# Rotary embedding of queries and keys: the swapped halves copied by DMA inside SBUF, with a signed sine table, instead of multiplied by a permutation matrix

## What is computed

```python
x = rms_norm(hidden_states, ln_in_w)
mixed = jnp.where(vm, x @ v_qkv, x @ l_qkv)
q, k, v = jnp.split(mixed, 3, axis=-1)
...
def rotate_half(x):
    d = x.shape[-1] // 2
    return jnp.concatenate([-x[..., d:], x[..., :d]], axis=-1)
...
q, k = q * cos + rotate_half(q) * sin, k * cos + rotate_half(k) * sin
```

## Time and profile before

| | us |
|---|---|
| median of three runs | 2036.79 |
| lowest and highest | 2032.74 and 2040.6 |
| the profiled execution | 2036.72 |
| its span | 2034.9 |
| PE busy | 1918.8 |
| DVE busy | 1113.8 |
| POOL busy | 887.1 |
| ACT busy | 830.2 |

### The profile page before, as it was taken

One profiled execution on the slowest core, in us unless ns is written; L12 is line 12 of the kernel. 1 busy time (PEld: TensorE's weight loads), 2 busy tenths in 40 slices (PEclk: granted clock), 3 DMA queues, 4 the chain that ended last, 5 costly groups with the idle time before them and its releaser, 6 DMA issues.

```text
span 2034.9 us, 35472 instructions
## 1 busy us (share of the span) xinstructions
PE 1918.8 (94%) x12620; PEld 1642.6 (81%) x12620; DVE 1113.8 (55%) x2663; ACT 830.2 (41%) x2198; POOL 887.1 (44%) x1037
## 2 busy tenths in 40 slices
PE   4999979997999999999999999998979999999998
PEld 3876767775999989888899879985458888887997
DVE  6777875666442553547676554222384766655422
ACT  2017526875211211256666423222235666652321
POOL 3340322341798999641121348840044212104884
PEclk9999988999999999999999999998989999999999
DMA  3110100010233333310000213322221000001332
GB/s 127 42 57 2 40 15 16 30 50 17 83 109 109 115 114 124 88 35 18 11 24 13 67 63 104 114 73 88 70 80 34 19 10 24 13 1 42 104 113 79
DMA packets 38190, 118.88 MB, mean 58 GB/s; under 512 B 6168, under 2 KB 10264, under 8 KB 38016
## 3 DMA queue, kind: packets, MB, share of 16 engines
q1 hardware_dynamic: 31408, 107.92, 17.3%
q10 hardware_dynamic: 6608, 8.68, 1.4%
HBM read 114.75 MB, written 1.84 MB: 57 GB/s over the span
## 4 chain that ended last, share of the span: by engine, by line
PE 82%; DVE 7%; POOL 5%; ACT 2%; issue 2%; DMA 1%; DVEq 0%; ACTq 0%; SPq 0%; POOLq 0%
PE psum L565 15%; PE psum L566 14%; PE psum L567 14%; PE psum L787 7%; PE psum L798 6%; PE psum L845 5%; PE psum L558 4%; PE psum L685 4%; PE psum L687 4%; PE psum L686 4%; POOL wl L1701 3%; DVE xc L1277 1%; DVE rstd L1262 1%; ACT probs_t L1042 1%; DVE total L1248 1%
## 5 line engine op out<-in xcount | busy, mean ns | idle before, releaser
L1701 POOL TENSOR_TENSOR wl<-raw,wh 128x256 fp32r<-128x256 f32 x656 | 518.9, 822 | 13.7
L565 PE MATMUL psum<-nh,wh 128*128 128x448 f32 x904 | 348.3, 385 | 15.3 <-DVEq L1477 8.0
L1693 POOL TENSOR_SCALAR wh<-raw 128x1024 fp32r<-128x1024 f32 x164 | 185.1, 1129 | 396.8 <-PE psum L567 158.4
L566 PE MATMUL psum<-nl,wh 128*128 128x448 f32 x904 | 336.9, 373 | 0.0
L567 PE MATMUL psum<-nh,wl 128*128 128x448 f32 x904 | 336.3, 372 | 0.0
L1042 ACT ACTIVATE probs_t<-masked_t,nmin 112x375 f32<-112x375 f32 (+1 forms) x384 | 202.6, 529 | 109.2 <-DVE nmin L1380 109.2
L1549 DVE TENSOR_TENSOR hid_l<-scr,hid_h 128x448 fp32r<-128x448 f32 x108 | 93.2, 863 | 229.0 <-ACT hid_h L1129 228.4
L565 PEld LDWEIGHTS psum<-nh,wh 128*128 128x128 f32 x904 | 174.7, 193 | 37.6 <-issue 12.5
L1380 DVE CUSTOM_DVE_ANT_0 masked_t<-psum,maskf 112x375 f32<-112x375 f32 x256 | 129.7, 544 | 116.9 <-PE psum L787 116.2
L798 PE MATMUL psum<-cst,probs_t 112*125 112x112 f32 (+1 forms) x1304 | 188.4, 274 | 3.8 <-ACT probsT_t L1069 3.4
L1069 ACT COPY probsT_t<-psum 125x336 f32<-125x336 f32 (+1 forms) x424 | 175.5, 456 | 40.4 <-PE psum L845 23.4
(11 more groups left out here) (182 smaller groups left out, 3861.9 us busy)
## 6 DMA issues: line engine op xcount, KB each, us to landing
raw<-in_walls SPq DMA_DIRECT2D x183, 512.0 KB, 3.5
raw<-in_ctxF SPq DMA_DIRECT2D x24, 375.0 KB, 3.0
ctxb<-in_ctxF ACTq DMA_DIRECT2D x8, 375.0 KB, 3.6
ctxt<-in_ctxK ACTq DMA_DIRECT2D x8, 375.0 KB
x<-in_xT ACTq DMA_DIRECT2D x2, 896.0 KB, 11.2
outT<-x SPq DMA_DIRECT2D x2, 896.0 KB, 5.1
mask<-in_kmask ACTq DMA_DIRECT2D x16, 41.0 KB, 2.6
vself<-in_tt SPq DMA_DIRECT2D x1, 448.0 KB, 6.5
```

The lines of the kernel that those rows point to most:

```text
L565: nc.tensor.matmul(out, ah, bh, start=(i == 0), stop=False)
L566: nc.tensor.matmul(out, ah, bl, start=False, stop=False)
L1693: nc.gpsimd.tensor_scalar(high, src, 1.0, 1.0, ALU.mult, ALU.mult).then_inc(split_h, 1)
L1701: last = nc.gpsimd.tensor_tensor(low[cut], src[cut], high[cut].bitcast(F32), ALU.subtract)
```

## The change

- PE's 16 products with `rot_w` are gone, and with them 16 places in the pool of three banks.
- In their place ACT issues eight DMAs for each tile (new function `rotate` in ACT's program), each copying 16 partitions of 448 floats (1792 bytes a partition) from `scr` to the neighbouring block of a new buffer `turned_qk`, 128 DMAs in all. ACT waits before each set of eight for `raw_qk` of that tile, and from the third set on for the rotation two tiles back.
- DVE multiplies `turned_qk` (SBUF) by the sines instead of PSUM, after a wait for the eight DMAs, and subtracts instead of adding.
- The signs go into the sine table: DVE sums `rot_w` by rows once (`sign`), and ACT scales the table by it when it copies it.
- `LATE`, `X_PART`, `x_whole` and `raw_turn` are new names without effect here, since `LATE` is empty and no normalisation uses the new parts.

```diff
@@ PE @@
-                    if name == "qk":
-
-                        if qk_seen[0] >= 1:
-                            rotate(qk_seen[0] - 1)
-                        qk_seen[0] += 1
...
-            def rotate(i):
-
-                pe.wait_ge(raw_qk, i + 1)
-                n = begin_tile(("rot", i), "dve")
-                nc.tensor.matmul(pool_bank(n)[:, 0:HALF], rot_w, scr[:, i % 2, :],
-                                 start=True, stop=True).then_inc(tile_ready, 1)
...
-            rotate(len(RAW) - 1)
@@ ACT @@
-                            nc.scalar.copy(dst[:, :], bank[:, 0:S]).then_inc(emptied["act"], 1)
+                            if i:
+                                act.wait_ge(sign_done, 1)
+                            nc.scalar.activation(dst[:, :], bank[:, 0:S], ACT.Copy, scale=sign[:, 0:1] if i else 1.0)\
+                                .then_inc(emptied["act"], 1)
...
-            stage("qk", None)
+            qk_seen = [0]
+
+            def rotate(half, m):
+
+                i = qk_seen[0]
+                qk_seen[0] += 1
+                act.wait_ge(raw_qk, i + 1)
+                if i >= 2:
+                    act.wait_ge(rope_done, i - 1)
+                for j in range(P // 16):
+                    act.dma_start(turned_qk[16 * j:16 * j + 16, i % 2, :], scr[16 * (j ^ 1):16 * (j ^ 1) + 16, i % 2, :])\
+                        .then_inc(turned_in[i % 2], 16)
+
+            stage("qk", rotate)
@@ DVE @@
+            nc.vector.tensor_reduce(sign[:, 0:1], rot_w, AX_X, ALU.add).then_inc(sign_done, 1)
...
                 link(nc.vector.tensor_mul(t, raw_t, cos))
-                dve.wait_ge(tile_ready, n + 1)
-                bank = pool_bank(n)[:, 0:HALF].rearrange("p (b s) -> p b s", b=BPH)
-                nc.vector.tensor_mul(dst, bank, sin).then_inc(emptied["dve"], 1)
-                dve.wait_ge(chain, links[0])
-                dve.wait_ge(emptied["dve"], count)
-                nc.vector.tensor_add(dst, dst, t).then_inc(rope_done, 1)
+                dve.wait_ge(turned_in[i % 2], 16 * (P // 16) * (i // 2 + 1))
+                other = turned_qk[:, i % 2, :].rearrange("p (b s) -> p b s", b=BPH)
+                dve.wait_ge(chain, link(nc.vector.tensor_mul(dst, other, sin)))
+                nc.vector.tensor_sub(dst, t, dst).then_inc(rope_done, 1)
```

More of the change, by code:

```diff
@@ L152 @@
 S_PART = {"s": range(KD), "s0": range(2), "s1": range(2, KD)}
+LATE = ()
+X_PART = {"x": range(KD), "x0": range(1), "x1": range(1, 2), "x2": range(2, 3), "x3": range(3, KD)}
 class PoolPlan:
@@ L262, in build @@
         ctxt = at("ctxt", [P, 4, CH * CC], F32, o_k)
+        turned_qk = at("turned_qk", [P, 2, HALF], F32, o_k + 8 * T)
+        assert 8 * T + 8 * HALF <= 4 * 4 * CH * CC
         place[0] = max(place[0], o_k + 4 * 4 * CH * CC)
@@ L299, in build @@
         eps = sb("eps", [P, 2])
+        sign = sb("sign", [P, 1])
         o_a = place[0]
@@ L346, in build @@
         raw_qk = sem("raw_qk")
+        turned_in = [sem(f"turned_in{i}") for i in range(2)]
+        sign_done = sem("sign_done")
         tile_ready = sem("tile_ready")
@@ L393, in build @@
         split_turn = {key: i for i, key in enumerate([o for o in order if o[0] != 5])}
+        raw_turn = {key: i for i, key in enumerate([o for o in order if o[0] != 5 and o[0] not in LATE])}
         def norm_done(eng, nn, half, k=KD - 1):
@@ L474, in build @@
             for it in SEQ[name]:
-                if it[0] == "norm" and it[3] in ("a", "s", "s0"):
-                    what = {"a": "m", "s": "v", "s0": "v"}[it[3]]
+                if it[0] == "norm" and it[3] in ("a", "s", "s0", "x", "x0"):
+                    what = "m" if it[3] == "a" else "v"
                     sums.append(({"m": "mean", "v": "var"}[what], it[1], it[2]))
@@ L506, in x_ready, with x_whole @@
                 tile_done(eng, (X_OF_NORM[nn], half, k))
+        def x_whole(eng, nn, half):
+            if nn == 0:
+                x_ready(eng, nn, half, 0)
+            else:
+                x_ready(eng, nn, half, KD - 1)
         def norm_src(nn):
@@ L604, in norm_part @@
                         .then_inc(tile_ready, 1)
-            qk_seen = [0]
             def tables():
@@ L984, in norm_part @@
                             continue
-                        act.wait_ge(nraw, split_turn[nn, half] * KD + k + 1)
+                        act.wait_ge(nraw, raw_turn[nn, half] * KD + k + 1)
                         if kind == "ln":
@@ L1480, in rope @@
                 _, half, m = RAW[i]
-                n, who, count = plan.tiles[("rot", i)]
-                given[0] += 1
-                assert count == given[0]
                 if i == 0:
```

## The result

| | us |
|---|---|
| before, median of 4 runs | 2037.0 (2032.7 to 2040.6) |
| after, median of 4 runs | 2054.9 (2051.1 to 2056.6) |
| ratio, 95% interval | 1.0085 (1.0063 to 1.0106) |
| after, span of the profiled execution | 2053.2 (before 2034.9) |

The changed kernel is 17.9 us slower, and its time lies above the range that was given (2030 to 2049).

What follows compares the result with a forecast made beforehand. PE was taken as the bound, 0.76 us of rotation in each 5.72 us tile. Start +2, middle -3.4 and end +1.8 summed to +0.4 us on 2036.72, given as 2037, range 2030 to 2049.

Steps and rivals of the forecast that it cites:

- What bounds the kernel: In the rotation stage PE sets the pace: a tile takes 4.96 us of products and 0.76 of rotation.
- The issue on ACT: On ACT's queue one copy issues in 0.37 us, a set of eight in 3.0, under PE's 4.96 a tile.
- The rival that the issue is the bound: On ACT's queue an issue costs 0.62 us, a set 5.0; sum +11.2 us, 2048; chance 0.18.
- Start: At the stage's start copy sets delay ACT's squares and root, so DVE reaches tile 2 at 58.3; net +2 us.
- Middle: Over twelve tile periods, 8 at 5.9 us beside POOL and 4 at 4.5, against 68.6 before: -3.4 us.
- End: At the stage's end the last swap arrives 5.6 us after the sum, scores start 8.4 after it: +1.8 us.
- The clock: While PE waits before the scores, a clock dip could add up to 2.7 us, counted only in the high end.
- Nothing behind the stage changes: After the rotation stage, no change from this edit was expected.
- Sum: Whole kernel: +2 - 3.4 + 1.8 = +0.4 us on 2036.72, given as 2037.
- The forecast's own high side: Whole kernel: the main case ends at +8 us, 2045; chance of that case 0.76.

Runs made afterwards that it cites:

- e2: Changed kernel without its 128 copies and the waits for them, DVE multiplying the unswapped `scr` by the sines: 2027.8 us, ratio to before 0.9957.
- e6: Changed kernel with copies split over ACT's and SP's queues, ACT's normalisation work moved ahead of the copy sets, and spare PE products: 2027.8 us, ratio to before 0.9950.
- e1: Changed kernel with 36 spare matmuls on PE in its wait before the scores: 2049.3 us, ratio to before 1.0065.
- e7: Changed kernel with four copies of 32 partitions a tile in place of eight of 16, halves landing in wrong blocks: 2032.6 us, one run.
- e3: Changed kernel with four of each tile's eight copies issued on SP's queue, four on ACT's: 2038.1 us, ratio to before 1.0002.
- e8: Changed kernel with the same eight copies a tile read from the input in HBM instead of `scr`: 2041.9 us, one run.
- e10: Kernel before with three spare reciprocals on DVE ahead of the last rotation, leaving PE idle: 2046.8 us, ratio to before 1.0042.
- e4: Changed kernel with ACT's squares of half 1 ahead of the first copy set, root and rounded copies ahead of the second: 2050.1 us, ratio to before 1.0067.
- e12: Changed kernel, unchanged, profiled once more: 2053.1 us, one run.

## Why the prediction was wrong, step by step

**What bounds the kernel (right).** PE sets the pace before, 0.76 us a tile belong to the rotation, and e2 gives all of it back between tile 2 and tile 15 (75.7 us to 65.5).

**The issue on ACT (the step that failed).** The prediction took 0.37 us for one of eight, between the first two rows, "since each copy has one run a partition", and kept 0.62 as an end. The runs show 0.61 to 0.64, whatever the partitions, on ACT's and on SP's queue. "3.0 is under 4.96, so its queue keeps up" is the sentence that fell with it: a set takes 5.0 us, a hair more than PE's 4.96, and the swaps become the bound of the stage. While POOL rests DVE could do a tile in 3.9 us, and yet tiles 8 to 11 are scaled at 96.14, 101.29, 106.41 and 111.52 us, 5.1 apart: there the sets follow each other on the queue with 0.1 us between them. Beside POOL it is not the queue alone. Four sets there (5, 6, 12 and 14) start only as DVE's sum ends, after 0.8 to 1.7 us without an issue. The pace is that of a round: issue a set (5.0), wait for its last landing (2.0 to 3.3), multiply, subtract, then scale and add the next tile. Two tiles took 13.1 us (4 to 6) and 11.6 (12 to 14), where the rival had reckoned 12.0 by the same round. The rival that the issue is the bound named the mechanism, the price and the sign, and had too little of a chance at 0.18.

**Start (+2 net forecast, of it +4.9 at tile 2; +9.1 measured there).** The chain of steps was right: squares behind set 0, root behind set 1. It put DVE at tile 2 at 58.3 with sets of 3.0 us; with the measured 5.1 and 5.0 it gives 58.3 + 4.1 = 62.4, and the trace has 62.50. Mis-sized were the issue and what was counted as given back: "net +2" rested on PE running ahead meanwhile, which is worth something only if DVE and the swaps can follow faster afterwards. They could not, as the swaps had no time to spare.

**Middle (-3.4 forecast, -4.0 measured from tile 2 to tile 15).** That the two numbers are close is luck. What the forecast counts as given back at the start (4.9 - 2 = 2.9 us) would show between tile 2 and tile 15, so by the same cut it had -6.3. And two errors in it go against each other. Beside POOL DVE needs 5.33 us a tile (e2), not 5.9, so the prediction charged 0.6 us too much for the reads from SBUF: in e2 the product with the cosines became cheaper (0.97 from start to start instead of 1.28) as the product with the sines became dearer (1.19 instead of 0.72). The starts alternate there, POOL's subtractions at 69.72, 70.67, 71.75 and 72.83 us, DVE's operations at 70.14, 71.11 and 72.30, so each seems to wait its turn. With the swap hidden the middle is -10.2 (e2) or -10.6 (e6). The swaps took the other 6 us.

**End (+1.8 forecast, +3.2 measured from tile 15 to the scores).** Within its ends (+1.3 to +5.3). The last set issues from the sum's end at 136.8 to 141.9, and the last copy takes 4.01 us to land, near the upper end taken, not 2.6. The swap is there 8.5 us after the sum, not 5.6.

**The clock (the second step that failed).** The text saw a dip coming and gave it "up to 2.7", by analogy with the one at 54 to 68 us, and put it into the high end only. It costs 6.9 us in one profile and 4.3 in the other (over 115.0), and roughly 5.5 by the medians of e1. "Nothing behind the stage changes" is true for the work and not for the clock it runs at.

**Sum.** At the first score product +0.4 was forecast and +8.3 measured; the rival had +11.2. With the 7.4 us of the self-attention in this profile (6.9 of the clock and 0.5 of unknown cause), which neither had, that makes the 15.7 us that are there when the scores end. The remaining 2.6 us of the profiled 18.3 are no more than what single profiles differ by.

**Range.** It reached to 2049 because the rival's low price was 2048. The rival's price had no clock in it; with 5.5 us it would have been 2053.5. The forecast's own high side was also added up too low: the ends +4, +1.4 and +5.3 make +10.7, not +8, and with the dip of 2.7 that the text allows it is +13.4, which is 2050.

## What to carry to other kernels

Price a swap by DMA by the number of its issues, not by its bytes: here 0.6 us for each copy out of SBUF on the queue that issues it, and then ask whether a set fits into the period of the loop, and which computation of the same engine stands behind it. Where PE is left idle ahead of a long stretch, count the slow clock behind it as well: here 1.4 to 6.9 us behind 5.9 to 7.7 us of idle, and different in two profiles of one kernel. A change that is slower as made may hold a gain: splitting the issues over two queues, moving ACT's own work ahead of them and keeping PE busy turned +0.85% into -0.5%.

## What the runs showed of the hardware

- The issue of a copy from SBUF to SBUF takes 0.61 us at the median on ACT's queue, with 16 partitions and with 32 of 1792 bytes each (after, e7), and 0.59 on SP's with 16 (e3); single issues took up to 2.19 (e7). From HBM the same copy takes 0.44 (e8). The landing of a copy from SBUF takes 2.0 us at the median (1.8 to 4.3). The prediction had 0.37 and 2.6.
- Idle times of 5.9 to 7.7 us brought the granted clock to 0.50 to 0.62, and the self-attention behind them took 1.4 us longer in e10 (over before's 114.55) and 4.1, 4.3, 4.3 and 6.9 in e4, e8, e12 and after (over 115.0). In e3 a wait of 2.49 us and one of 1.10 soon after it went with 4.4. In e7 one of 2.80 us, and in e2 one of 2.79 and one of 0.23, went with none, since the clock was back by about the first score product. The Trainium skill, TensorE: Matmul & The Clock Gate, section Why this matters for your kernels, warns of idle gaps between bursts of matmuls, since the engine goes back to its lower clock. The traces agree, since the granted clock fell to 0.62 or below behind each of these waits, and add that what it costs varies, by 2.6 us between two profiles of the same kernel.
- Beside POOL's subtractions three two-input operations of DVE in a row take 0.97, 1.19 and 0.97 us, where alone they take 0.55 to 0.65. A third such operation in the tile cost only 0.24 us more than the two of before (5.33 against the 5.09 of the earlier trace rows).
